# An attention kernel with its side work re-planned: second norms in two parts, tokens copied out of PSUM, pieces gathered beside the GELU

## The chip, the cores and the metric

The kernel runs on one core of a Trainium2 chip. The metric is the device time of one execution in microseconds (us). Three executions of the kernel before took 2359.71, 2360.52 and 2369.72 us; the median is 2360.52.

## The reference

The input `x` holds 8 waveforms (the batches) of 120000 samples, each cut into 1500 frames of 80. D is 256, everything is float32. Cut to what is computed:

```python
h = layernorm(einsum('bfr,hr->bfh', frames, W) + b) * gamma + beta
h = gelu(h)                                    # tokens, 8 x 1500 x 256
z = layernorm(h)
Q, K, V = heads(z @ Wq.T + bq), heads(z @ Wk.T + bk), heads(z @ Wv.T + bv)  # 16 heads of 16
h = h + join(softmax(Q @ K.T / 4) @ V) @ Wo.T + bo         # 1500 x 1500 per head
t = layernorm(h)                               # the third stage takes 8 // 16 = 0 tokens
out = h + layernorm(t) * ln_g + ln_b           # per head, so its norm alone is left
```

## The kernel before

**Tiling.** A batch of 1500 tokens is 12 tiles (`NT`) of 125 (`T`) or 3 chunks (`NC`) of 500 (`QC`). The 16 heads form 4 groups of 4. A *unit* is one group of heads against one chunk of queries: 12 units a batch (u = 0 to 11), 96 in all. A unit has 24 *slots* (`WIN`, k = 0 to 23). In slot k TensorE computes the scores of slot k + 1, two heads against one tile of keys, into two PSUM banks of four (`scores`, L972), ScalarE takes the exponential of 125x1000 numbers (L537), and on even slots TensorE multiplies the probabilities of two finished slots into the attended heads (`attend`, L1002), two further banks.

**Side work.** Everything else is cut into *pieces* that a table `PLAN[u, k]` puts into odd slots, written by hand with `place(u, what, (k, i), ...)`. A piece with several steps takes a step every second slot (`OFFSETS`). The pieces are: `tok` i, two tiles of tokens of a later batch; `turn` i, transposes of two tiles of z; `qk` i, a projection of one chunk to Q (even i) or K (odd i), i below 6 for the first two groups of heads, from 6 on for the last two; `norm` and `flag`, sums of squares and a bound for the softmax's scale; `val` i, values of a tile; `out` i, the output projection of a tile of the batch in front. TensorE runs them in `beside` (L1006). Pieces of units 5 to 11 mostly belong to the next batch. All pieces of a unit use one pair of PSUM banks, the pair in which the unit in front gathered its attended heads. So a piece waits until VectorE has freed the piece in front of it (`s_free`), and the first piece of a unit waits until `take_sums` has read the pair (`s_ov`).

**VectorE** goes through the same table, in order: in slot 1 `take_sums` (L669, L671), in slot 7 `invert` (L675), in slot 12 `normalise` (L679, L681), and for the last step of each piece `tok_stats` and `tok_norm` (L567 to L583), `take_turn` (L608), `take_qk` (L619, L621: the float16 high and low half), `take_val` (L628), `take_norm`, `take_flag` (L643 on) and `take_out` (L688 to L694), whose end `finish_out` (L702) follows three slots later. After `take_sums` the second norm of the next batch stands at the places in `NORMS`: `norm_stats` (L591, L594), then a wait for the root that GpSimd computes (L408, L410), then `norm_apply` (L600), one chunk at a time.

**ScalarE** takes the GELU of the next batch, all twelve tiles, at unit 4, slot 2 (`GELU`), with a table load in front and behind; TensorE has nothing in its program for that time.

**SP** issues the DMAs, in one order too: the sums go out to a thin layout (`spread_sums`, L300, slot 1) and back as reciprocals (`gather_sums`, L304, slot 7); four stores bring the attended heads to `oT` (`store_attended`, L315, slot 12); the halves of a projection go to DRAM (L281) and come back in the layout that scores need by eight loads (`lay_out`, L295), three slots later. Before the first unit of each half batch TensorE waits for those loads (`laid_out`).

**The start** makes the tokens of batch 0 and its first six projections with whole pieces, four pairs of banks in turn; VectorE takes all of them, and ScalarE is idle after its GELUs until the first scores.

## Time and profile before

| | |
|---|---|
| median of three executions | 2360.52 us |
| the profiled execution | 2361.47 us, of which its span is 2359.7 |
| ScalarE busy | 2134.5 us (90%) |
| TensorE busy | 2080.5 us (88%) |
| VectorE busy | 963.5 us (41%) |
| GpSimd busy | 394.8 us (17%) |
| TensorE's mean granted clock | 0.966 |
| chain that ended last | ScalarE 40%, TensorE 27%, issue 13%, VectorE 7% |

Times in the rows count from the start of the span. A group of instructions has its busy time, its mean in ns, and the idle time of its engine before it with what ended most of it. Busy shares are means over all stages. Where two engines are both near 90%, the question is which waits for which, and in which unit.

### The profile page before, as it was taken

To read this page: it belongs to the slowest core of one execution; us is meant where nothing else is said; L and a number is where in the kernel's file an instruction comes from. 1 tells how busy PE (TensorE), PEld (TensorE's weight loads), DVE (VectorE), ACT (ScalarE), POOL (GpSimd) and SP (SyncE) were. 2 spreads that over 40 slices of the span, in tenths; PEclk is the share of its full clock that TensorE was granted. 3 is DMA by queue.
4 is the path that set the end of the run, shared out by engine and by line. 5 is a ranking of instruction groups with operands and counts; after the bars stand their busy time and mean duration, and the time that the engine had idled before them with its cause. 6 is when DMAs were issued, how large, how long until landed. Compare 5 with 4: busy or idle time off the path is not lost.

```text
span 2359.7 us, 123320 instructions
## 1 busy us (share of the span) xinstructions
PE 2080.5 (88%) x56576; PEld 902.7 (38%) x56576; DVE 963.5 (41%) x2261; ACT 2134.5 (90%) x2334; POOL 394.8 (17%) x637
## 2 busy tenths in 40 slices
PE   4798999889998899988999799998999889999885
PEld 1432444333433344433444344443444333433223
DVE  6443335452344424444345433454335453343214
ACT  1498999989999899998999899998999989999993
POOL 2211102130122201222012210222102130011003
PEclk7998999999999999999999999999999999999997
DMA  2311211212121120221212112121211203122001
GB/s 71 81 45 42 56 42 46 56 31 75 32 57 48 44 67 22 59 64 43 62 25 57 53 48 58 35 58 38 66 41 48 53 23 78 28 58 57 18 10 35
DMA packets 114866, 113.91 MB, mean 48 GB/s; under 512 B 41003, under 2 KB 110698, under 8 KB 114338
## 3 DMA queue, kind: packets, MB, share of 16 engines
q1 hardware_dynamic: 111802, 104.10, 17.3%
q8 instruction: 446, 7.31, 1.3%
q10 hardware_dynamic: 2536, 1.83, 0.3%
q14 instruction: 82, 0.67, 0.1%
HBM read 55.16 MB, written 36.86 MB: 39 GB/s over the span
## 4 chain that ended last, share of the span: by engine, by line
ACT 40%; PE 27%; issue 13%; DVE 7%; SPq 5%; DMA 4%; POOL 2%; DVEq 2%; POOLq 0%
ACT prob L537 39%; PE PS L1002 12%; PE PS L972 7%; SPq L295 3%; DMA qk_halves_scratch<-HL 3%; PE PS L924 2%; SPq L315 1%; PE PS L871 1%; PE PS L909 1%; PE PS L894 1%; DMA oT<-Osb 1%; DVE Hs L576 1%; DVE z L600 1%; DVE Den L679 1%; POOL Hs L418 1%
## 5 line engine op out<-in xcount | busy, mean ns | idle before, releaser
L537 ACT ACTIVATE prob<-PS 125x1000 f32<-125x1000 f32 x2304 | 2089.7, 1070 | 155.9 <-PE PS L972 151.2
L1002 PE MATMUL PS<-prob,Vst 64*17 64x500 f32 (+1 forms) x18432 | 1214.7, 587 | 1.6 <-issue 0.8
L972 PE MATMUL PS<-QA,KA 64*32 64x500 f16 (+1 forms) x18432 | 958.9, 381 | 132.4 <-ACT prob L537 124.5
L972 PEld LDWEIGHTS PS<-QA,KA 64*32 64x32 f16 (+1 forms) x18432 | 276.8, 90 | 1054.0 <-ACT prob L537 1004.2
L1002 PEld LDWEIGHTS PS<-prob,Vst 61*17 61x17 f32 (+1 forms) x18432 | 341.3, 93 | 42.2 <-issue 9.0
L619 DVE TENSOR_SCALAR HL<-PS,b_qk 128x500 f16<-128x500 f32 x96 | 70.9, 739 | 459.4 <-PE PS L894 453.2
L894 PE MATMUL PS<-zT,w_qk 64*32 64x250 f32 x5760 | 229.4, 372 | 15.0 <-DVE Hs L576 8.5
L426 POOL TENSOR_TENSOR sq<-HL 128x500 bf16<-128x500 f16 x96 | 98.1, 1022 | 861.1 <-DVE HL L621 761.1
L924 PE MATMUL PS<-w_o,oT 64*32 64x128 f32 (+1 forms) x6144 | 129.9, 279 | 38.7 <-DVE Hs L576 27.9
L433 POOL TENSOR_TENSOR Y<-Hs,be_ln 125x256 f32<-125x256 f32 x96 | 70.3, 732 | 540.3 <-DVE Hs L688 529.5
L909 PE MATMUL PS<-w_v,zT 64*32 64x128 f32 (+1 forms) x5376 | 116.9, 280 | 34.2 <-DVE nrow L643 33.6
L894 PEld LDWEIGHTS PS<-zT,w_qk 64*32 64x32 f32 x5760 | 107.5, 106 | 70.8 <-DVE Hs L576 12.1
L924 PEld LDWEIGHTS PS<-w_o,oT 64*32 64x32 f32 (+1 forms) x6144 | 99.8, 108 | 88.6 <-DVE Hs L576 41.5
L909 PEld LDWEIGHTS PS<-w_v,zT 64*32 64x32 f32 (+1 forms) x5376 | 91.8, 109 | 66.2 <-DVE nrow L643 36.8
L688 DVE TENSOR_TENSOR Hs<-Hs,PS 125x256 f32<-125x256 f32 x96 | 40.3, 420 | 186.9 <-PE PS L924 186.9
L669 DVE COPY Osb<-PS 128x500 f32<-128x500 f32 x96 | 64.5, 672 | 117.9 <-PE PS L1002 116.4
L628 DVE TENSOR_TENSOR Vst<-PS,b_v 125x256 f32<-125x256 f32 x96 | 39.8, 419 | 160.4 <-PE PS L909 159.5
L871 PE MATMUL PS<-w_tok,X 40*32 40x256 f32 (+3 forms) x1536 | 68.2, 405 | 13.6 <-DMA w_tok<-in_tok_b 9.5
L418 POOL TENSOR_TENSOR Hs<-Hs,b_o 125x256 f32<-125x256 f32 x96 | 71.5, 775 | 31.4 <-DVE z L600 31.4
L675 DVE RECIPROCAL thin<-thin 100x20 f32<-100x20 f32 x96 | 26.5, 276 | 119.8 <-DMA thin<-Osb 119.8
L621 DVE SCALAR_TENSOR_TENSOR HL<-PS,b_qk,HL 128x500 f16<-128x500 f32 x96 | 71.0, 739 | 7.5 <-issue 0.4
L681 DVE TENSOR_TENSOR Osb<-Den,Osb 128x500 f32<-128x500 f32 x96 | 68.3, 712 | 7.5 <-issue 0.4
(83 smaller groups left out, 968.9 us busy)
## 6 DMA issues: line engine op xcount, KB each, us to landing
qk_halves_scratch<-HL SPq DMA_DIRECT2D x96, 250.0 KB, 2.3
QA<-qk_halves_scratch SPq DMA_DIRECT2D x384, 62.5 KB
KA<-qk_halves_scratch SPq DMA_DIRECT2D x384, 62.5 KB
oT<-Osb SPq DMA_DIRECT2D x384, 31.2 KB, 2.0
out<-Y SPq DMA_DIRECT2D x24, 500.0 KB
X<-in_x SPq DMA_DIRECT2D x16, 234.4 KB
thin<-Osb SPq DMA_DIRECT2D x96, 7.8 KB
Den<-thin SPq DMA_DIRECT2D x96, 7.8 KB
```

Of the source, the lines that this page charges most:

```text
L295: sp.dma_start(dst[to:to + HD, 2 * m:2 * m + 2, :, k * QC:(k + 1) * QC], src[par])\
L418: ins = pool.tensor_tensor(h, h, b_o[:, :], ALU.add)
L426: pool.tensor_tensor(sq[:, p % 2, :], HL[:, p % 3, 0, :], HL[:, p % 3, 0, :], ALU.mult).then_inc(s_sq, 1)
L537: act.activation(prob[0:T, 2 * (w % 6):2 * (w % 6) + 2, :], PS[0:T, 2 * (w % 2):2 * (w % 2) + 2, 0:QC], ACT.Exp, scale=scl)\
L619: dve.tensor_scalar(hi, both, bias, None, ALU.add)
L621: dve.scalar_tensor_tensor(out=lo, in0=both, scalar=bias, in1=hi, op0=ALU.add, op1=ALU.subtract)\
L871: last = pe.matmul(PS[lo:hi, bank + j, 0:D], X[rows, 2 * i + j, lo:hi], w_tok[rows, :], start=(step == 0), stop=(step == 1))
L894: last = pe.matmul(PS[lo:hi, bank + j, 0:QC // 2], w_qk[rows, c, w, m * 128 + lo:m * 128 + hi], zT[rows, c, k * QC + j * QC // 2:k * QC + ...
L909: last = pe.matmul(PS[lo:hi, bank + j, 0:D // 2], zT[rows, c, t + lo:t + hi], w_v[rows, c, j * D // 2:(j + 1) * D // 2], start=(step == 0 ...
L924: last = pe.matmul(PS[lo:hi, bank + j, 0:D // 2], oT[rows, c, oslot(b, e // CT), e % CT * T + lo:e % CT * T + hi], w_o[rows, c, j * D // 2 ...
L972: last = pe.matmul(PS[lo:hi, bank, 0:QC], KA[rows, G % NG, h // 2, t * T + lo:t * T + hi], QA[rows, G % NG, h // 2, c * QC:(c + 1) * QC], ...
L1002: last = pe.matmul(PS[lo:lo + HD + 1, bank + r, 0:QC], Vst[rows, b % 2, t, g * HG + j, :], prob[rows, (HG * t + j) % 12, :], start=(t == 0 ...
```

## The change

- The norm is split: `norm_stats` and the root in `STATS`, `norm_apply` and the bias in `APPLY`, with slots between them, in units 4 and 5.
- Tokens of batches after the first are copied from PSUM to SBUF first, which frees the banks; statistics and the subtraction read the copy.
- `gather_in` puts outputs 9 and 10 and projection 11, all steps, into the even slot 2 of unit 4, where the GELU stands. `beside` is now called in every slot, after `attend`.
- Most other pieces change place. Outputs 0 to 3 are all in unit 11, tokens 0 and 1 in units 9 and 10, turns in units 4 and 5.
- `lay_out` of finished projections is issued in slot 13, after the stores of attended heads, no longer three slots after the projection.
- At the start ScalarE takes the turns' copies and the high halves, with a semaphore for each (`s_zt`, `s_hi`), and issues the loads of odd projections. `FREED` counts the pieces that VectorE frees, since these turns no longer count in `s_free`.

The diff, without the semaphores' bookkeeping: everywhere else `s_free` is waited for with `FREED[n]` instead of `n`.

```diff
+    def gather_in(u, k, what, *at):
+        for i in at:
+            for step in range(len(OFFSETS[what])):
+                PLAN[u, k].append((what, i, step, step == len(OFFSETS[what]) - 1))
+    GELU = (4, 2)
+    STATS = {(4, 5): 0, (4, 10): 1, (4, 18): 2}
+    APPLY = {(4, 8): 0, (4, 17): 1, (5, 4): 2}
     place(0, "qk", (3, 6), (17, 7))
-    place(0, "out", (13, 3))
+    place(0, "out", (13, 4))
     place(1, "norm", (3, 3))
-    place(1, "out", (5, 4), (13, 5))
+    place(1, "out", (5, 5), (13, 6))
     place(1, "tok", (9, 2))
     place(1, "qk", (17, 8))
-    place(2, "out", (5, 6), (13, 7))
+    place(2, "out", (5, 7), (13, 8))
     place(2, "tok", (9, 3))
     place(2, "qk", (17, 9))
     place(3, "norm", (3, 4))
-    place(3, "tok", (5, 4), (13, 5))
-    place(3, "out", (9, 8))
+    place(3, "tok", (5, 4), (11, 5))
     place(3, "qk", (17, 10))
-    place(4, "out", (5, 9), (9, 10))
-    place(4, "qk", (17, 11))
+    gather_in(4, 2, "out", 9, 10)
+    gather_in(4, 2, "qk", 11)
+    place(4, "out", (7, 11))
+    place(4, "turn", (13, 0), (15, 1), (21, 2), (23, 3))
     place(5, "norm", (3, 5))
-    place(5, "turn", (5, 0), (7, 1))
-    place(5, "out", (9, 11))
-    place(5, "flag", (13, 1))
-    place(5, "val", (15, 0), (19, 1))
-    place(6, "turn", (3, 2), (5, 3))
-    place(6, "qk", (7, 0), (17, 1))
+    place(5, "flag", (7, 1))
+    place(5, "turn", (9, 4), (11, 5))
+    place(5, "val", (13, 0), (17, 1), (21, 2))
+    place(6, "qk", (3, 0), (17, 1))
+    place(6, "val", (13, 3))
     place(7, "norm", (3, 0))
-    place(7, "val", (5, 2), (13, 3))
-    place(7, "turn", (9, 4), (11, 5))
+    place(7, "val", (5, 4), (9, 5), (13, 6))
     place(7, "qk", (17, 2))
-    place(8, "qk", (3, 3), (17, 4))
-    place(8, "val", (13, 4))
+    place(8, "val", (5, 7), (9, 8), (13, 9))
+    place(8, "qk", (17, 3))
     place(9, "norm", (3, 1))
-    place(9, "val", (5, 5), (9, 6), (13, 7))
-    place(9, "qk", (17, 5))
-    place(10, "norm", (3, 2))
-    place(10, "val", (5, 8), (11, 9), (15, 10), (19, 11))
-    place(10, "flag", (9, 0))
-    place(11, "tok", (3, 0), (11, 1))
-    place(11, "out", (7, 0), (15, 1), (19, 2))
-    assert all(len(steps) < 1 + k % 2 for (u, k), steps in PLAN.items())
-    NORMS = {(4, 12): 0, (5, 12): 1, (6, 8): 2}
-    GELU = (4, 2)
+    place(9, "val", (5, 10), (9, 11))
+    place(9, "tok", (13, 0))
+    place(9, "qk", (17, 4))
+    place(10, "tok", (5, 1))
+    place(10, "qk", (17, 5))
+    place(11, "norm", (3, 2))
+    place(11, "out", (5, 0), (13, 1), (17, 2), (21, 3))
+    place(11, "flag", (9, 0))
+    assert all(len(steps) < 1 + k % 2 or (u, k) == GELU for (u, k), steps in PLAN.items())
...
-            return b + 2 if u >= NU - 2 else b + 1
+            return b + 2 if u >= NU - 3 else b + 1
...
+    FREED, TURNED = [0], [0]
+    for what, pb, i in USE:
+        turned = (what, pb) == ("turn", 0)
+        FREED.append(FREED[-1] + (not turned))
+        TURNED.append(TURNED[-1] + turned)
...
+        def lay_out(eng, b, i):
+            p, k, w, m = nth(b, i), chunk_of(i), i % 2, i // (2 * NC)
+            dst = KA if w else QA
+            eng.wait_ge(s_st[p % 3], at(s_st[p % 3], 16 * (p // 3 + 1)))
+            if p >= 4 * NC or second[0]:
+                eng.wait_ge(s_sc, at(s_sc, max(0, WIN * NC * 2 * (p // (2 * NC) - 1))))
+            for par in range(2):
+                for blk in range(4):
+                    to, half_ = 64 * par + HD * blk, blk // 2 if w else blk % 2
+                    src = qk_s[b, i, :, half_, :].rearrange("(a two r) q -> two r a q", two=2, r=HD)
+                    eng.dma_start(dst[to:to + HD, 2 * m:2 * m + 2, :, k * QC:(k + 1) * QC], src[par])\
+                      .then_inc(s_ld, 16)
...
                 for i in range(2 * NC):
                     store_halves(0, i)
-                    if i > 0:
-                        lay_out(0, i - 1)
-                lay_out(0, 2 * NC - 1)
+                    if i % 2:
+                        lay_out(sp, 0, i - 1)
...
-                        if stored and stored[0][0] == WIN * n + k:
-                            lay_out(*stored.pop(0)[1:])
...
                         if k == NORMALISE + 1:
+                            while stored:
+                                lay_out(sp, *stored.pop(0))
                             if u == 4 and b + 2 < B:
                                 load_x(b + 2)
-                            if u in (1, 3, 6) and b > 0:
-                                store_out(b - 1, u // 2 if u < 6 else 2)
+                            if u in (0, 2, 5) and b > 0:
+                                store_out(b - 1, (u + 1) // 2 if u < 5 else 2)
...
-                                stored.append((WIN * n + k + 3, pb, i))
+                                stored.append((pb, i))
...
+                            if b + 1 < B and (u, k) in STATS:
+                                root2(b + 1, STATS[u, k])
+                            if b + 1 < B and (u, k) in APPLY:
+                                add_bias(b + 1, APPLY[u, k])
...
+            def turn_out(i):
+                act.wait_ge(s_full, at(s_full, USE["turn", 0, i] + 1))
+                bank = pair(USE["turn", 0, i])
+                act.activation(zT[:, :, i * 2 * T:(i + 1) * 2 * T], PS[:, bank:bank + 2, 0:2 * T], ACT.Copy)\
+                   .then_inc(s_zt, 1)
+            def high_half(i):
+                p, w, bank = nth(0, i), i % 2, pair(USE["qk", 0, i])
+                if p >= 3 or second[0]:
+                    act.wait_ge(s_st[p % 3], at(s_st[p % 3], 16 * (p // 3)))
+                    act.wait_ge(s_sq, at(s_sq, max(0, p - 2)))
+                act.wait_ge(s_full, at(s_full, USE["qk", 0, i] + 1))
+                act.activation(HL[:, p % 3, 0, :].rearrange("p (a q) -> p a q", a=2), PS[:, bank:bank + 2, 0:QC // 2],
+                               ACT.Identity, bias=b_qk[:, w * KC:w * KC + 1]).then_inc(s_hi, 1)
...
+                for k in range(NC):
+                    for j in range(2 * k, 2 * k + 2):
+                        turn_out(j)
+                    for i in range(2 * k, 2 * k + 2):
+                        high_half(i)
+                        if i > 0 and i % 2 == 0:
+                            lay_out(act, 0, i - 1)
+                lay_out(act, 0, 2 * NC - 1)
...
+            def fresh(b, i):
+                return Hs[:, hslot(b, 2 * i):hslot(b, 2 * i) + 2, :]
             def tok_stats(b, i):
                 p, tok = i % 2, two(USE["tok", b, i], slice(0, T), D)
                 dve.wait_ge(s_full, at(s_full, USE["tok", b, i] + 1))
+                if b > 0:
+                    dve.tensor_copy(fresh(b, i), tok).then_inc(s_free, 1)
+                    dve.drain()
+                    tok = fresh(b, i)
...
+                if b > 0:
+                    tok = fresh(b, i)
...
-                ins.then_inc(s_free, 1)
+                if b == 0:
+                    ins.then_inc(s_free, 1)
...
-                if p >= 3 or second[0]:
+                if (p >= 3 or second[0]) and p >= 2 * NC:
                     dve.wait_ge(s_st[p % 3], at(s_st[p % 3], 16 * (p // 3)))
...
-                dve.tensor_scalar(hi, both, bias, None, ALU.add)
+                if p < 2 * NC:
+                    dve.wait_ge(s_hi, at(s_hi, p + 1))
+                else:
+                    dve.tensor_scalar(hi, both, bias, None, ALU.add)
...
+                    if b + 1 < B and (u, k) in STATS:
+                        norm_stats(b + 1, STATS[u, k])
+                    if b + 1 < B and (u, k) in APPLY:
+                        norm_apply(b + 1, APPLY[u, k])
...
-                    if finish and finish[0][0] == k:
+                    if finish and finish[0][0] <= k:
...
-                    for j in range(2):
-                        take_turn(0, 2 * k + j)
...
+            def turned(b, i):
+                if b == 0:
+                    pe.wait_ge(s_zt, at(s_zt, i + 1))
+                else:
+                    pe.wait_ge(s_free, at(s_free, FREED[USE["turn", b, i] + 1]))
...
-                        pe.wait_ge(s_free, at(s_free, use))
+                        pe.wait_ge(s_free, at(s_free, FREED[use]))
...
-                    if k % 2:
-                        beside(b, u, k)
-                    elif k:
+                    if k % 2 == 0 and k:
                         attend(n, k // 2 - 1)
-                    elif n > 0:
+                    elif k == 0 and n > 0:
                         attend(n - 1, NT - 1)
+                    beside(b, u, k)
...
-                    pe.wait_ge(s_free, at(s_free, use - reach + 1))
+                    pe.wait_ge(s_free, at(s_free, FREED[use - reach + 1]))
+                    if use < FIRST and TURNED[use - reach + 1]:
+                        pe.wait_ge(s_zt, at(s_zt, TURNED[use - reach + 1]))
```

## Rows read from the trace of the kernel before

**Rows 1.** Costliest groups: line, operation, count | busy, mean ns | idle before, releaser

```profile
L537 ACT ACTIVATE prob<-PS 125x1000 f32<-125x1000 f32 x2304 | 2089.7, 1070 | 155.9 <-PE PS L972 151.2
...
L619 DVE TENSOR_SCALAR HL<-PS,b_qk 128x500 f16<-128x500 f32 x96 | 70.9, 739 | 459.4 <-PE PS L894 453.2
```

**Rows 2.** Timeline of ScalarE, last batch: start us, length us, what, [idle before]

```profile
2089.71 230.17 ACT L537 ACTIVATE prob<-PS 125x1000 f32<-125x1000 f32 x256 [0.43 <-PE PS L972]
```

**Rows 3.** ScalarE's windows of units 1+2, 3+11, 4, 5, 7, batches 0-6: sums

```profile
sum 315.91, ACT 304.60; mean ACT 21.76
...
sum 326.87, ACT 307.14; mean ACT 21.94
...
sum 200.96, ACT 190.40; mean ACT 27.20
...
sum 202.32, ACT 155.03; mean ACT 22.15
...
sum 165.76, ACT 154.39; mean ACT 22.06
```

**Rows 4.** The same for units 0, 6, 8, 9 and 10 together

```profile
605.63:627.39 21.76, 21.71 (x25) 1.00 0.18 46
...
sum 761.76, ACT 756.47; mean ACT 21.61
```

**Rows 5.** Timeline of ScalarE at the GELU of batch 1

```profile
459.36 1.28 ACT L530 ACT_TABLE_LOAD   x1
...
464.82 3.69 ACT L537 ACTIVATE prob<-PS 125x1000 f32<-125x1000 f32 x4
```

**Rows 6.** Timeline of VectorE and TensorE, batch 1, unit 5

```profile
500.46 1.40 DVE L591 BATCH_NORM_STATS2 st<-Hs 125x6 f32<-125x256 f32 x4
...
503.86 1.38 DVE L600 TENSOR_SCALAR z<-Hs,mv,rs 125x256 f32<-125x256 f32 x4 [1.55 <-POOL rs L410]
...
505.42 1.11 PE L909 MATMUL PS<-w_v,zT 64*32 64x128 f32 x32 [5.10 <-DVE nrow L643]
```

**Rows 7.** Timeline of VectorE and TensorE behind a token piece, batch 1, unit 1

```profile
399.98 0.77 DVE L567 BATCH_NORM_STATS2 st<-PS 125x6 f32<-125x256 f32 x2 [0.86 <-PE PS L871]
...
402.09 0.67 PE L924 MATMUL PS<-w_o,oT 64*32 64x128 f32 x32 [0.88 <-DVE Hs L576]
...
404.56 0.42 DVE L688 TENSOR_TENSOR Hs<-Hs,PS 125x256 f32<-125x256 f32 x1
...
405.51 0.64 PE L894 MATMUL PS<-zT,w_qk 64*32 64x250 f32 x16
...
405.85 0.48 DVE L694 SCALAR_TENSOR_TENSOR hg<-Hs,mv,g_ln 125x256 f32<-125x256 f32 x1
```

**Rows 8.** Timeline of TensorE behind the GELU of batch 1

```profile
465.88 0.61 PE L972 MATMUL PS<-QA,KA 64*32 64x500 f16 x8 [5.24 <-ACT prob L537]
```

**Rows 9.** Timeline of VectorE, a turn's copy at the start

```profile
44.13 0.68 DVE L608 COPY zT<-PS 128x500 f32<-128x500 f32 x1 [0.15 <-PE PS L880]
```

**Rows 10.** Timeline of VectorE, the sums' second step, batch 1, unit 4

```profile
460.13 0.68 DVE L671 TENSOR_TENSOR Osb<-Osb,PS 128x500 f32<-128x500 f32 x1
```

**Rows 11.** Timeline of VectorE, normalise in batch 1, unit 10

```profile
618.21 0.01 DVE L679 LOAD_MASK_SELECT Den<-Den  x1 [1.83 <-DMA Den<-thin]
...
619.01 0.68 DVE L681 TENSOR_TENSOR Osb<-Den,Osb 128x500 f32<-128x500 f32 x1
```

**Rows 12.** Timeline of SP's issues: start, last to first scores, stores, loads

```profile
83.24 3.70 SPq L295 DMA_DIRECT2D KA<-qk_halves_scratch  x8
...
404.60 2.45 SPq L315 DMA_DIRECT2D oT<-Osb  x4
...
610.01 6.20 SPq L295 DMA_DIRECT2D KA<-qk_halves_scratch  x8
```

**Rows 13.** Loads by line L295: engine, times as min/median/max ns

```profile
L295 SPq DMA_DIRECT2D QA<-qk_halves_scratch x384: 302/426/2057, 53.1 to 2158.9; - x192
```

**Rows 14.** Timeline of TensorE, the first scores

```profile
88.81 1.03 PE L972 MATMUL PS<-QA,KA 64*32 64x500 f16 x16 [7.57 <-DMA KA<-qk_halves_scratch]
```

More of the change, by code:

```diff
@@ L887, in project @@
                 if step == 0:
-                    pe.wait_ge(s_free, at(s_free, USE["turn", b, 2 * k + 1] + 1))
+                    turned(b, 2 * k + 1)
                 begin("qk", b, i, step)
@@ L901, in values @@
                 if step == 0:
-                    pe.wait_ge(s_free, at(s_free, USE["turn", b, i // 2] + 1))
+                    turned(b, i // 2)
                 begin("val", b, i, step)
@@ L1106, in run @@
                 pe.wait_ge(s_wo, 16 * 5)
[L1107 removed]
+                pe.wait_ge(s_free, at(s_free, FREED[FIRST]))
                 for b in range(B):
```

34 lines of the change are left out of this document (8 added, 26 removed).

## The prediction

> **What bounds the kernel now.** I read the costliest groups of the page first. ScalarE computes 2304 exponentials that cover 2089.7 us of the 2359.7 us span, and almost all of its idle time there, 151.2 us, is waiting for TensorE's scores (L972) [rows 1]. So ScalarE sets the pace, and the question is what a unit of 24 exponentials costs against its floor. The floor is in the last batch, where 256 exponentials run without a gap in 230.17 us, 0.899 each, 21.58 a unit [rows 2]. Next I cut ScalarE's time into units, the same unit of batches 0 to 6 together, and took the floor (7 x 21.58 = 151.05, twice that for a pair of units) from each sum [rows 3, 4]. Lost in seven batches: units 1 and 2 together 13.8 us, units 3 and 11 together 24.8, unit 4 12.3 (after 7 x 5.37 for GELU and its two table loads: 5.46 from 459.36 to 464.82 [rows 5], less 0.09 that the last exponential in front saves in overlap), unit 5 51.3, unit 7 14.7, and the five others 6.5. That is 123 us. The last batch loses nearly nothing. The start, up to the first scores, is looked at by itself; the tail behind the last exponential is not touched. These 123 us are all that the middle can give.
>
> The cause of each loss is in the timelines of TensorE and VectorE. In unit 5 TensorE stands 5.10 us before a value piece, because VectorE is in the second norm (statistics, 1.55 us waiting for GpSimd's root, application) and reaches the flag row only then [rows 6]. TensorE then works at half clock (1.11 us for a half piece of values). After every token piece it stands 0.88 us, since the two PSUM banks come free only after statistics and subtraction [rows 7]; there are six token pieces a batch, two each in units 3 and 11, one each in 1 and 2. At the GELU TensorE is idle for 5.24 us [rows 8] and starts again at half clock.
>
> **The change part by part.** I follow one batch, in the frame of batch 1, with the durations of its rows.
>
> *Unit 5.* Norm statistics and application are split and moved to units 4 and 5, so that the root is ready when VectorE comes back, and flag and turns no longer follow a norm. Between the pieces left in unit 5 VectorE has under 2 us of work each. Of 51.3 I leave 1.4: -49.9.
>
> *Unit 7.* There two turns were mixed with values, and the sums were spread behind eight loads on SP. Now it holds values (one 0.4 us VectorE step each), and the loads come after the attended heads. Of 14.7 I leave 0.5: -14.2.
>
> *Tokens.* A copy of two banks costs about 0.68 [rows 9] and frees them after 0.8 us instead of 2.1. The price is 0.68 more on VectorE for each pair. In unit 3 and in units 9 and 10, where the pieces of unit 11 go, the next piece is four slots off or VectorE has room: the token stalls of units 3 and 11 go, of their 24.8 I leave 1 (-23.8), to which unit 11's new wait is added below. In units 1 and 2 the order stays token, normalise, output, projection. From the start of statistics (399.98) to the freeing of the output piece (L688 ends 404.98) VectorE takes 5.0 us [rows 7]; with the copy 5.7. TensorE wants that pair for the projection 4.65 us after the same point (it came at 405.51, 5.53 later, and 0.88 of that is the wait that now goes). So it waits 1.1 us one piece later, where it waited 1.1 before: 13.8 becomes 13.3 (-0.5). On reading from SBUF: four statistics from SBUF take 1.40 us, 0.35 each [rows 6], two from PSUM 0.77 [rows 7], 0.38 each, so the copy earns back at most 0.1 us.
> The Trainium skill (VectorE: DVE Perf Modes, "The TRN2 errata") charges a VectorE instruction 58 cycles plus its elements from SBUF and 120 from PSUM, at 0.96 GHz; by that, four later reads would earn back an estimated 0.26 us and units 1 and 2 would end some 3 us lower. The row speaks for less.
>
> *The burst at GELU.* Slot 2 of unit 4 now holds outputs 9 and 10 and projection 11, in one row, on one pair of banks. TensorE can start when the sums are taken, 460.8 [rows 10]. An output piece is two steps of 0.65, a projection four of 0.64 [rows 7]; each next piece waits about 0.6 for VectorE's take of 0.42. 460.9 + 1.35 + 0.6 + 1.3 + 0.6 + 2.6 = 467.4. Scores for the fifth exponential of the unit then come at 467.4 rather than when the bank is free (465.9), so ScalarE waits about 1.15 us, but at full clock; before, the slow restart cost most of unit 4's 1.76 (12.3 over 7).
> Behind it VectorE carries a backlog: take 11 (L619 and a second step like it, 0.74 each [rows 1]) to 469.2, statistics 1.8 to 471.1, two finishes 1.0, reciprocal 0.3, application 1.4 from the root at 472.7 to 474.1, output 11 1.8 (as L688 to the end of L694 [rows 7]), statistics 1.8, normalise 1.5, a finish 0.5: 479.6, and only then turn 0, whose banks TensorE wants for turn 1 at 478.3. Free at 480.3: a wait of 2.0, of which 1.85 reaches ScalarE. So unit 4 costs 3.1 us in batches 1 to 6 and about 0.8 in batch 0 (no outputs yet): 19.4 for 12.3, +7.1. Bounds 12 and 30: no backlog at all, or each application with the 2 us that it has beside GpSimd work.
> In batch 7 the same three pieces stand in slot 2 with no GELU above them. TensorE leaves the slot 6.7 us late and nothing hides it: +6.7.
>
> *Loads behind attended heads.* This is a new wait. Projection 5 of the next batch ends at slot 23 of unit 10, and its eight loads go out at slot 13 of unit 11, in SP's order behind the four stores of attended heads, which wait for VectorE's normalise. In unit 10 of before (starts 605.63 [rows 4]) normalise began at 618.21, 1.83 of it waiting for the sums' DMA [rows 11], which now is not behind loads. With an output instead of a value (+0.3) and a finish (+0.5) it ends 13.0 us after the unit's start. Stores 2.45, loads 4.6 (6.2 in the longest group [rows 12], 3.4 if all eight take the median of 0.43 [rows 13]), landing 1.9 (the last issue before the first scores ended at 86.94, the scores began at 88.81 [rows 12, 14]): 22.0. TensorE wants them 20.8 us in. So each of seven hand-overs waits 1.2 us, of which 1.1 counts, 7.7, with small stalls +8.2. Bounds: 0 and 2.7 each, 19 in all. For units 6 to 11 the loads go out in unit 4, early enough.
>
> *The start.* ScalarE takes turn copies and high halves, VectorE the low halves. Equal cost, but eight loads are issued on ScalarE between high halves 2 and 3, and again between 4 and 5. No row shows loads issued there; I take SP's 4.6 for eight, 3.4 and 6.2 as its ends. High half 3 slips by 3 us, and with it norm, turns and projection 4, high half 5 by 6. Against that the last loads no longer queue behind five others: TensorE waited 7.57 us for them [rows 14]. My chain gives the last landing at 89.3 for 88.8: +0.5, bounds -2 and +4.
> The Trainium skill (DMA: Bandwidth & Descriptors, "Issuing engines are not separate DMA queues") says that a second issuing engine saves only the issuing time. That is all that I count here.
>
> The other five units: -1 (one token stall in batch 0). Sum: -49.9 -14.2 -23.8 -0.5 +7.1 +6.7 +8.2 +0.5 -1.0 = -66.9. The profiled execution took 2361.5 (span 2359.7 and 1.8 around it), the median is 0.95 lower: 2360.5 - 67 = 2294 with rounding.
>
> **Rivals.** (A) The clock falls in the burst. TensorE pauses four times for banks while the sequence runs. At half clock a half piece costs 1.11 [rows 6] instead of 0.65; eight steps make 3.8 us a batch, some 26 in all: 2320. For it: the clock did fall after 5.24 us idle. Against it: no pause in the burst is over 0.7 us, and after the pause of 0.88 us the output step took 0.67, full speed [rows 7].
> The Trainium skill (TensorE: Matmul & The Clock Gate, "A second HAM failure mode: psum-queue depth-cycling") has this very case, short idles between groups that wait for PSUM banks. By that rule this rival would hold.
> (B) VectorE becomes the bound wherever a copy was added, as I expect it in units 1 and 2 only: units 3, 9 and 10 would then keep the 1 us per token piece, four a batch, and the turns wait 2 us in batch 0 too: +28 +2, 2324. Against it: there the pieces stand four slots apart.
> (C) The change does not do what it says: the unit 5 stall is the flag's own chain (take, transposes), not the norm in front. Then about 4 of 7.3 us stay: 2294 + 28 = 2322. The rows speak against it: the norm ends at 505.24, and TensorE starts at 505.42 [rows 6].
> (D) Slower: loads right behind the stores fill the ring. The longest single load issue lasted 2.06 us [rows 13]. If all eight took that, the hand-over would come 16.5 - 4.6 = 11.9 us later, 83 us in seven, and the time is 2377. It decides from 11.3 us each (67 + 12 = 79 over 7). Only single loads were that slow, so it is unlikely.
>
> **How the numbers follow.** Forecast 0.62, A 0.12, B 0.1, C 0.06, in between or a stall that I have not seen 0.06, D 0.04. The forecast's own bounds: down 7 (unit 4), 8 (hand-over) and 2 (start); up 11, 11 and 4. Not all at once: 2278 to 2310. The range takes in A, B and C: 2277 to 2326. A measurement can tell about 0.5%, 12 us, from no change. Faster by over that 0.91, within 0.05, slower 0.04.
>
> **What would show it.** Right: in unit 5 ScalarE's windows sum to 153 rather than 202 and no 5 us wait before a value piece; in unit 3 no idle between token and next piece; in units 1 and 2 the idle has moved from the output to the projection; one gap of 6 to 7 us in batch 7, unit 4; a wait for turn 0's banks in unit 4; TensorE waits for KA or QA at the end of unit 11. A shows as half clock (1.2 GHz) in the stretch behind GELU. I am wrong if VectorE's chain with the copy is not 5.7 us, or if the loads need clearly more or less than 4.6.

## The result, and the profile after

The changed kernel took 2303.92 us (median of 4 executions, 2301.73 to 2309.14), the kernel before 2360.11 beside it: a ratio of 0.9757 (95% interval 0.9726 to 0.9788), 56 us less. The forecast was 2294 in a range of 2277 to 2326, and faster. The profiled execution took 2301.73 (2361.47 before): 59.7 less, where the sum said 66.9. So the time fell in the range, and 7 to 10 us of the forecast gain are missing.

The page after. Columns are those of [rows 1]: busy time, mean in ns, idle time before and what ended most of it.

```profile
span 2299.7 us, 123422 instructions
PE 2071.1 (90%) x56576; PEld 871.5 (38%) x56576; DVE 974.5 (42%) x2291; ACT 2131.7 (93%) x2346; POOL 393.4 (17%) x637
...
ACT 51%; PE 22%; issue 10%; DVE 6%; SPq 3%; POOL 2%; DMA 2%; DVEq 2%; POOLq 1%; ACTq 0%
...
L579 ACT ACTIVATE prob<-PS 125x1000 f32<-125x1000 f32 x2304 | 2079.5, 1086 | 69.3 <-PE PS L1034 66.7
```

ScalarE's idle time ahead of the exponentials (L537 before, L579 now) fell from 155.9 to 69.3 us, of which TensorE's scores end 66.7. Some 38 of that fall is no gain: ahead of the first exponential the row counts 49.7 us before and 11.2 after, since ScalarE now has work at the start, while that exponential came only 1.4 us sooner. The other 48 lie between the exponentials, and their busy time fell by 10 (from 2089.7), as one that follows a stop takes longer: 1.00 us alone and about 0.91 in a row. The number of exponentials is the same, and ScalarE's part in the chain that ended last rose from 40% to 51%. VectorE has 11 us more to do: its 42 token copies take 28.6, and against them stand the six turn copies and six high halves that went to ScalarE (8.5) and smaller differences.

ScalarE's windows of batches 0 to 6, cut as in [rows 3, 4]: units 1 and 2, units 3 and 11, unit 4, unit 5, unit 7, then the five others. The first number is the length of all windows together, to be set against the floor of 151.05 a unit.

```profile
sum 313.06, ACT 304.38; mean ACT 21.74
...
sum 317.39, ACT 303.38; mean ACT 21.67
...
sum 212.16, ACT 192.63; mean ACT 27.52
...
sum 154.39, ACT 152.70; mean ACT 21.81
...
sum 151.85, ACT 151.64; mean ACT 21.66
...
sum 759.92, ACT 753.61; mean ACT 21.53
```

Less the floor, and 37.6 for GELU and tables in unit 4, beside the sum of the prediction (differences are taken before rounding). "Hand-over" is the wait at the end of unit 11 for the loads that the next batch's first scores need:

| term | before | after | measured | predicted |
|---|---|---|---|---|
| unit 5 | 51.3 | 3.3 | -47.9 | -49.9 |
| unit 7 | 14.7 | 0.8 | -13.9 | -14.2 |
| units 3 and 11 (tokens go, hand-over comes) | 24.8 | 15.3 | -9.5 | -23.8 + 8.2 |
| units 1 and 2 | 13.8 | 11.0 | -2.8 | -0.5 |
| unit 4, batches 0 to 6 | 12.3 | 23.5 | +11.2 | +7.1 |
| unit 4, batch 7 | 0 | 7.1 | +7.1 | +6.7 |
| the five others | 6.5 | 4.7 | -1.8 | -1.0 |
| first exponential | 89.5 | 88.1 | -1.4 | +0.5 |

With -1.0 in the rest of batch 7 and in the tail these make the 60.0 by which the span fell. A window of one unit alone, unit 3, sums to 151.17: of 15.3 in units 3 and 11, 15.2 is the hand-over in unit 11. Two terms are too small in the forecast, hand-over by 7 and unit 4 by 4, and the five others hide a stall that was not foreseen: unit 0 rose from 2.8 to 7.3 over eight batches, while the rest fell.

The granted clock changed too. Before, TensorE fell to half clock (1.2 GHz) once in unit 4 and once in unit 5 of batches 0 to 6; the mean of those windows was 0.88 or 0.89 (0.94 in unit 5 of two batches), as in batch 1's unit 5:

```profile
485.80:515.36 29.56, 22.22 (x26) 0.88 0.14 35
```

After, both units stand at 1.00 in every batch. So what unit 5 gained is the wait and the slow restart behind it.

What stands behind each, in timelines (start, length, idle before and its end). Batch 1, unit 4, on ScalarE behind the GELU and its table load (to 450.62), then TensorE's burst and VectorE beside it:

```profile
450.63 1.90 ACT L579 ACTIVATE prob<-PS 125x1000 f32<-125x1000 f32 x2
454.01 11.83 ACT L579 ACTIVATE prob<-PS 125x1000 f32<-125x1000 f32 x13 [1.48 <-PE PS L1034]
```

```profile
446.67 1.47 PE L986 MATMUL PS<-w_o,oT 64*32 64x128 f32 x64 [0.22 <-DVE Osb L728]
448.72 1.46 PE L986 MATMUL PS<-w_o,oT 64*32 64x128 f32 x64 [0.58 <-DVE Hs L745]
450.76 3.00 PE L956 MATMUL PS<-zT,w_qk 64*32 64x250 f32 x64 [0.58 <-DVE Hs L745]
```

The pauses between the three pieces are 0.58 us, as the 0.6 of the prediction; a piece of output takes 1.47 rather than 1.35 and the projection 2.8 up to the next scores (453.55), not 2.6. So the exponentials wait 1.48 here and at most 1.57 in batches 1 to 6, not 1.15. The granted clock through the burst was 1.00, which is 2.4 GHz:

```profile
447.00:451.00 4.00, 2.58 (x132) 1.00 0.03 6
451.00:455.00 4.00, 3.63 (x96) 1.00 0.02 4
```

(window, its length, TensorE busy, granted clock, DMA share, GB/s). Rival A needed half clock there and falls.

Unit 4 loses 3.84 us in each of batches 1 to 6: this wait, 1.6 ahead of turn 1, which waits for turn 0's banks (forecast 1.85), and some 0.7 that is in neither. ScalarE's own busy time is 27.5 to 27.6 a unit there, where floor and GELU make 26.95 (27.2 before). The runs don't take that part apart.

In batch 7 there is no GELU above the burst, and in unit 1 the wait moved to the projection:

```profile
2094.91 5.49 ACT L579 ACTIVATE prob<-PS 125x1000 f32<-125x1000 f32 x6 [7.07 <-PE PS L1034]
```

```profile
387.74 0.69 DVE L614 COPY Hs<-PS 125x512 f32<-125x512 f32 x1 [0.74 <-PE PS L927]
388.52 0.75 DVE L618 BATCH_NORM_STATS2 st<-Hs 125x6 f32<-125x256 f32 x2
...
393.01 0.41 DVE L745 TENSOR_TENSOR Hs<-Hs,PS 125x256 f32<-125x256 f32 x1
```

```profile
393.48 0.66 PE L956 MATMUL PS<-zT,w_qk 64*32 64x250 f32 x16 [0.92 <-DVE Hs L745]
```

From the start of the copy (387.74) to the end of the step that frees the output's pair (393.42) VectorE takes 5.7 us, which is the 5.7 of the prediction, and TensorE waits 0.92 for it. No other token piece has a wait over 0.5 us behind it.

The hand-over at the end of batch 1's unit 11, which starts at 603.7 (VectorE, SP, TensorE; the scores feed unit 0 of the next batch):

```profile
616.23 0.68 DVE L738 TENSOR_TENSOR Osb<-Den,Osb 128x500 f32<-128x500 f32 x1
```

```profile
616.94 3.27 SPq L332 DMA_DIRECT2D oT<-Osb  x4
620.31 4.59 SPq L299 DMA_DIRECT2D KA<-qk_halves_scratch  x8
```

```profile
626.78 0.40 PE L1034 MATMUL PS<-QA,KA 64*32 64x500 f16 x8 [1.58 <-DMA KA<-qk_halves_scratch]
```

Normalise ends 13.2 us into the unit here, 12.9 to 13.5 in the seven (13.0 forecast). The four stores took 3.27, 3.0 in the mean (2.45 forecast), the eight loads 4.59 here, but 4.5 to 6.4 in the seven and 5.0 in the mean (4.6 forecast). The scores start 23.1 us into the unit here and 23.3 in the mean, where the chain gave 22.0. TensorE waits 1.58 us for them here, 1.2 to 3.2 in the seven; the longest wait stands behind the longest loads (batch 4).

The stall in unit 0 that was not in the sum, batch 1 (VectorE, then TensorE):

```profile
355.63 0.48 DVE L751 SCALAR_TENSOR_TENSOR hg<-Hs,mv,g_ln 125x256 f32<-125x256 f32 x1
356.58 0.48 DVE L759 SCALAR_TENSOR_TENSOR Y<-hg,rs,Y 125x256 f32<-125x256 f32 x1 [0.46 <-POOL rs L454]
357.01 0.68 DVE L726 COPY Osb<-PS 128x500 f32<-128x500 f32 x1
357.76 0.68 DVE L728 TENSOR_TENSOR Osb<-Osb,PS 128x500 f32<-128x500 f32 x1
```

```profile
358.49 0.66 PE L956 MATMUL PS<-zT,w_qk 64*32 64x250 f32 x16 [1.22 <-DVE Osb L728]
```

Output 3 has its second step in slot 23 of unit 11. Its take and its finish, which waits 0.46 us for GpSimd's root, stand on VectorE ahead of `take_sums`, and the first piece of unit 0 needs the pair that `take_sums` reads.

### The profile page after: what moved, and what is told of

Read it like the earlier page. It is cut to its first block, busy times and chain, and to the rows that moved or that the text cites. A ratio compares the mean times of both kernels' runs of the same rounds, so it can differ in the third digit from the quotient of the medians.

```text
span 2299.7 us, 123422 instructions
## 1 busy us (share of the span) xinstructions
PE 2071.1 (90%) x56576; PEld 871.5 (38%) x56576; DVE 974.5 (42%) x2291; ACT 2131.7 (93%) x2346; POOL 393.4 (17%) x637
## 4 chain that ended last, share of the span: by engine, by line
ACT 51%; PE 22%; issue 10%; DVE 6%; SPq 3%; POOL 2%; DMA 2%; DVEq 2%; POOLq 1%; ACTq 0%
ACT prob L579 51%; PE PS L1064 9%; PE PS L1034 5%; PE PS L956 2%; PE PS L986 2%; SPq L299 2%; DMA thin<-Osb 1%; PE PS L971 1%; SPq L332 1%; PE PS L936 1%; DVE Den L736 1%; DMA KA<-qk_halves_scratch 1%; DVE Hs L745 1%; DVEq L746 1%; DVEq L727 1%
## 5 line engine op out<-in xcount | busy, mean ns | idle before, releaser
L579 ACT ACTIVATE prob<-PS 125x1000 f32<-125x1000 f32 x2304 | 2079.5, 1086 | 69.3 <-PE PS L1034 66.7
L1064 PE MATMUL PS<-prob,Vst 64*17 64x500 f32 (+1 forms) x18432 | 1190.4, 580 | 0.7 <-ACT prob L579 0.6
L1034 PE MATMUL PS<-QA,KA 64*32 64x500 f16 (+1 forms) x18432 | 934.4, 377 | 121.9 <-ACT prob L579 107.5
L1034 PEld LDWEIGHTS PS<-QA,KA 64*32 64x32 f16 (+1 forms) x18432 | 263.7, 89 | 1086.6 <-ACT prob L579 1054.8
L1064 PEld LDWEIGHTS PS<-prob,Vst 61*17 61x17 f32 (+1 forms) x18432 | 333.5, 93 | 35.8 <-issue 4.5
L450 POOL TENSOR_TENSOR Y<-Hs,be_ln 125x256 f32<-125x256 f32 x96 | 70.5, 734 | 437.7 <-DVE Hs L745 437.7
L986 PE MATMUL PS<-w_o,oT 64*32 64x128 f32 (+1 forms) x6144 | 125.3, 275 | 17.4 <-DMA oT<-Osb 9.0
L956 PEld LDWEIGHTS PS<-zT,w_qk 64*32 64x32 f32 x5760 | 101.5, 105 | 89.3 <-DVE Hs L745 22.5
L986 PEld LDWEIGHTS PS<-w_o,oT 64*32 64x32 f32 (+1 forms) x6144 | 95.4, 107 | 50.8 <-issue 10.7
L971 PE MATMUL PS<-w_v,zT 64*32 64x128 f32 (+1 forms) x5376 | 110.5, 269 | 0.6 <-issue 0.6
L435 POOL TENSOR_TENSOR Hs<-Hs,b_o 125x256 f32<-125x256 f32 x96 | 68.2, 743 | 78.5 <-DVE z L654 78.5
L927 PE MATMUL PS<-w_tok,X 41*32 41x256 f32 (+3 forms) x1536 | 65.5, 408 | 13.6 <-DMA w_tok<-in_tok_b 9.9
```

Source lines behind the costliest of these rows:

```text
L435: ins = pool.tensor_tensor(h, h, b_o[:, :], ALU.add)
L450: pool.tensor_tensor(Y[:, k % 2, e % CT, :], Hs[:, hslot(b, e), :], be_ln[:, :], ALU.add)
L579: act.activation(prob[0:T, 2 * (w % 6):2 * (w % 6) + 2, :], PS[0:T, 2 * (w % 2):2 * (w % 2) + 2, 0:QC], ACT.Exp, scale=scl)\
L956: last = pe.matmul(PS[lo:hi, bank + j, 0:QC // 2], w_qk[rows, c, w, m * 128 + lo:m * 128 + hi], zT[rows, c, k * QC + j * QC // 2:k * QC + ...
L971: last = pe.matmul(PS[lo:hi, bank + j, 0:D // 2], zT[rows, c, t + lo:t + hi], w_v[rows, c, j * D // 2:(j + 1) * D // 2], start=(step == 0 ...
L986: last = pe.matmul(PS[lo:hi, bank + j, 0:D // 2], oT[rows, c, oslot(b, e // CT), e % CT * T + lo:e % CT * T + hi], w_o[rows, c, j * D // 2 ...
```

## The experiments

All kernels below compute everything. "Unit sums" are what ScalarE loses against the floor in that unit, added over the eight batches; for the changed kernel, units 0 to 5 and 11: 7.3, 5.8, 5.0, 0.0, 30.6, 3.3, 15.3. They scatter where an edit can't reach: unit 11 lost 13.1 to 18.5 in the kernels that leave its pieces and loads alone, and batch 0's units 0 and 4 vary by 1 to 2.5 us with a fall to half clock that some executions have there. The kernel before took 2357.86, 2360.48 and 2358.54 us beside the three groups of runs.

### Without the copy of the tokens

```diff
-                if b > 0:
-                    dve.tensor_copy(fresh(b, i), tok).then_inc(s_free, 1)
-                    dve.drain()
-                    tok = fresh(b, i)
...
```

> The changed kernel without the copy of the tokens: statistics and subtraction read PSUM again. Theory (spacing): what took the token stalls out of unit 3 is that the next piece stands four slots behind the token, not the copy. Without the copy a wait of 1 us comes back only where the next piece is two slots off and VectorE's queue is short: unit 9 in six batches, and twice in batch 0; in units 1 and 2 the wait moves from the projection back to the output at the same size. 2304 + 8 = 2312 us. Rival (copy, as the prediction had it): units 3 and 9 to 11 get their waits back, four a batch, some 2330 us.

Measured 2318.21 us, ratio 0.9829 (0.9794 to 0.9863). Units 1 and 2 lose the same with and without the copy (5.7 and 4.8); without it TensorE waits one piece earlier, at the output:

```profile
399.11 0.67 PE L979 MATMUL PS<-w_o,oT 64*32 64x128 f32 x32 [0.87 <-DVE Hs L623]
```

Unit 3 goes from 0.0 to 3.8, unit 9 from -0.5 to 5.1. That is 9.4 us by the copy. Start, hand-over and unit 4, which this edit should not touch, add 1.8, 2.5 and 2.2, and unit 0 adds 2.0, all of it in batch 0 (2.0 for -0.2; four kernels that keep the copy lose 1.1 to 1.3 there), so of the 14 us between the medians some are scatter. I had unit 9 in my 8, and not unit 3. Of the 13.3 us that unit 3 lost before, 3.8 come back without the copy; the other 9.5 went with its new plan, which spaces the pieces and has one output less. The prediction had put all under one term, without a share for either.

### The split alone, in the kernel before

```diff
-    NORMS = {(4, 12): 0, (5, 12): 1, (6, 8): 2}
+    STATS = {(4, 12): 0, (5, 8): 1, (6, 6): 2}
+    APPLY = {(4, 15): 0, (5, 11): 1, (6, 9): 2}
...
```

A split can't leave both halves in place: the applications move by one to three slots, the statistics by up to four.

> The kernel before with the norm split alone: statistics at slots (4,12), (5,8), (6,6), application at (4,15), (5,11), (6,9), everything else as it was. Theory (norm in front of the flag): VectorE reaches the flag at 501.6 in the frame of batch 1 instead of 505.2, TensorE waits 1.6 us instead of 5.1 and keeps its clock; unit 5 loses 10 us in seven batches instead of 51: 2360 - 41 = 2319 us. Rival (the flag's own chain and the turns hold TensorE): some 4 of 7.3 us a batch stay, 2338 us.

Measured 2330.37 us, 0.988 (0.9844 to 0.9916). Unit 5 falls from 51.2 to 19.4, so the second norm in front was about 32 of the 48 us that the whole change took out there, and the flag's own chain (rival C) at most the rest. The slow restart went with the long wait: the granted clock in unit 5 is 1.00 in six of seven batches, for 0.88 to 0.94 before. What is left is again VectorE's order, shown in batch 1 by the application and the flag row:

```profile
493.71 1.38 DVE L602 TENSOR_SCALAR z<-Hs,mv,rs 125x256 f32<-125x256 f32 x4 [1.55 <-POOL rs L411]
...
498.60 0.20 DVE L645 COPY nrow<-PS 1x64 f32<-1x64 f32 x1
```

```profile
498.86 0.67 PE L912 MATMUL PS<-w_v,zT 64*32 64x128 f32 x32 [1.79 <-DVE nrow L645]
```

The 1.55 us for GpSimd's root are still waited for with three slots between the halves. Application, a take of output and normalise then stand ahead of the flag row. The split needs the new places to be worth all of it.

### The new places, norms whole

```diff
-    STATS = {(4, 5): 0, (4, 10): 1, (4, 18): 2}
+    STATS = {(4, 8): 0, (4, 17): 1, (5, 4): 2}
```

Statistics now stand in the slot of their application.

> The changed kernel with the norm whole again: statistics at the slots of the applications, (4,8), (4,17), (5,4), so VectorE waits 1.5 us for each root. Theory (place counts, split little): in unit 5 the flag comes four slots after the norm, so only 0.7 us a batch comes back there, and about 1.4 us before turn 2 in unit 4, less 0.6 that turn 0 gains: 2304 + 9 = 2313 us. Rival (the split itself removed the stall of unit 5): 5 us a batch come back in unit 5, 2339 us.

Measured 2337.86 us, 0.9912 (0.9885 to 0.994). I was wrong: not 9 but 34 us over the changed kernel. Unit 5 loses 12.5 (3.3 with the split), but unit 4 takes most, 53.6 for 30.6. VectorE, GpSimd and ScalarE of batch 2:

```profile
743.89 1.38 DVE L654 TENSOR_SCALAR z<-Hs,mv,rs 125x256 f32<-125x256 f32 x4 [1.54 <-POOL rs L427]
...
750.44 0.48 DVE L759 SCALAR_TENSOR_TENSOR Y<-hg,rs,Y 125x256 f32<-125x256 f32 x1 [1.57 <-POOL rs L454]
```

```profile
745.35 2.98 POOL L435 TENSOR_TENSOR Hs<-Hs,b_o 125x256 f32<-125x256 f32 x4 [1.50 <-DVE z L654]
748.29 1.16 POOL L450 TENSOR_TENSOR Y<-Hs,be_ln 125x256 f32<-125x256 f32 x1
...
749.86 0.55 POOL L454 TENSOR_TENSOR rs<-rs,mhalf 125x1 f32<-125x1 f32 x1
```

```profile
753.09 1.00 ACT L579 ACTIVATE prob<-PS 125x1000 f32<-125x1000 f32 x1 [4.27 <-PE PS L1034]
```

A second cost of a late application shows here. Behind it GpSimd adds the bias (L435) for 2.98 us, then output 11's own addition (L450, 1.16 us), and only then comes the root of output 11 (L454). VectorE stands 1.57 us in `finish_out` for this root, and turn 0 is next on VectorE. No run takes the root ahead of L450. TensorE's wait for turn 0, 3.8 us, also brought it to half clock: unit 4's windows stand at 0.94 or 0.95 here and at 1.00 in the changed kernel, so a part of the 23 us of unit 4 is the slow restart.

### Who holds turn 0 in unit 4

```diff
-    STATS = {(4, 5): 0, (4, 10): 1, (4, 18): 2}
+    STATS = {(4, 5): 0, (4, 14): 1, (4, 18): 2}
```

The prediction saw turn 0 behind VectorE's backlog: here the second statistics (1.8 us) go behind turn 0.

> The changed kernel with the second chunk's statistics at (4,14) instead of (4,10), behind turn 0 on VectorE. Theory (backlog in front of turn 0): the wait of 1.7 us at slot 17 of unit 4 goes in six batches: 2304 - 10 = 2294 us. Rival (VectorE is short of time in the whole unit): the 1.8 us are missing at turn 2 or at the sums of unit 5 instead, 2304 us.

Measured 2302.64 us, 0.9764 (0.9736 to 0.9791): no gain. The rival had the time right, but not the cause: nothing went missing at turn 2 or in unit 5 (2.5 for 3.3), the wait for turn 0's banks stayed where it was. VectorE, GpSimd and ScalarE of batch 2:

```profile
738.29 1.08 DVE L738 TENSOR_TENSOR Osb<-Den,Osb 128x500 f32<-128x500 f32 x1
740.95 0.48 DVE L759 SCALAR_TENSOR_TENSOR Y<-hg,rs,Y 125x256 f32<-125x256 f32 x1 [1.58 <-POOL rs L454]
741.35 0.67 DVE L662 COPY zT<-PS 128x500 f32<-128x500 f32 x1
```

```profile
738.80 1.17 POOL L450 TENSOR_TENSOR Y<-Hs,be_ln 125x256 f32<-125x256 f32 x1
...
740.37 0.55 POOL L454 TENSOR_TENSOR rs<-rs,mhalf 125x1 f32<-125x1 f32 x1
```

```profile
743.13 3.85 ACT L579 ACTIVATE prob<-PS 125x1000 f32<-125x1000 f32 x4 [1.72 <-PE PS L1034]
```

VectorE had nothing to do for 1.58 us and waited for GpSimd's root. So my backlog was only one of two holders of equal length. The next kernel keeps this edit and moves the finish of output 11 behind turn 0 too:

```diff
-                            finish.append((k + 3, pb, i))
+                            finish.append((k + 5 if u == 4 and i == NT - 1 else k + 3, pb, i))
```

> The changed kernel with the second chunk's statistics at (4,14) as in the run before, and with the finish of output 11 two slots later (slot 14, behind turn 0). Theory (GpSimd's queue): output 11's root waits on GpSimd behind the 3 us of the first chunk's bias, VectorE waits for that root in its finish, and turn 0 stands behind the finish. With the finish behind turn 0 and the statistics too, nothing is in front of it: the wait of 1.8 us at slot 17 of unit 4 goes in six batches, 2303 - 10 = 2293 us. Rival (VectorE's own instructions, normalise above all, end too late anyway): it stays, 2303 us.

Measured 2295.18 us, 0.9732 (0.9713 to 0.9751); unit 4 falls from 31.4 (with the statistics moved alone) to 22.1. In batches 1 to 6 it is 1.8 us each in all but one (3.97 to 2.14), as expected; batch 0 gives 1.1 back, with half clock behind its GELU. Turn 0's copy now follows the normalise:

```profile
738.68 1.08 DVE L738 TENSOR_TENSOR Osb<-Den,Osb 128x500 f32<-128x500 f32 x1
739.69 0.67 DVE L662 COPY zT<-PS 128x500 f32<-128x500 f32 x1
```

The wait for GpSimd's root is shown as the second holder. The pair of edits gains; the finish without the statistics was not run.

### The burst of three outputs, and its copy in batch 7

```diff
-    gather_in(4, 2, "out", 9, 10)
-    gather_in(4, 2, "qk", 11)
-    place(4, "out", (7, 11))
+    gather_in(4, 2, "out", 9, 10, 11)
+    place(4, "qk", (3, 11))
...
+                            if len(finish) == 2:
+                                finish_out(*finish.pop(0)[1:])
```

> The changed kernel with outputs 9, 10 and 11 beside the GELU and projection 11 in slots 3 to 9, of unit 4. Theory (length of the burst): three outputs need 1.3 + 0.6 + 1.3 + 0.6 + 1.3 = 5.1 us from 460.9, so TensorE is back at 466.0 when the bank is free; the wait at slot 4 shrinks from 1.7 to 0.3 in six batches and from 7.3 to 5.7 in batch 7, and VectorE has 1 us less of backlog before turn 0: 2304 - 8 - 2 - 5 = 2289 us. Rival (VectorE's three output chains bind): the banks come free later, projection 11 waits, and the unit costs what it did: 2304 us.

Measured 2295.59 us, 0.9731 (0.9704 to 0.9759). Unit 4 falls from 30.6 to 20.6. After the tables ScalarE waits 0.43 us and not 1.48 (batch 1):

```profile
459.27 2.86 ACT L578 ACTIVATE prob<-PS 125x1000 f32<-125x1000 f32 x3
462.56 8.33 ACT L578 ACTIVATE prob<-PS 125x1000 f32<-125x1000 f32 x9 [0.43 <-PE PS L1035]
```

Two things changed at once: the burst is 1.3 us shorter, and output 11 is out of the way of turn 0, behind which ScalarE waits 0.44 to 0.62 us and no longer 1.6. Batches 1 to 6 lose 1.9 each for 3.84, batch 7 6.3 for 7.1; batch 0 loses 2.4 more, at half clock. Each of the two waits fell by 1.0 to 1.2. The medians differ by 8.3 us, for 10 in unit 4.

The last batch with its four pieces spread over slots 3 to 21 again:

```diff
...
+        for what, i, step, last in SPREAD.get(k, []) if (b, u) == (B - 1, 4) else PLAN[u, k]:
```

> The changed kernel, where the last batch, which has no GELU, runs outputs 9 to 11 and projection 11 of unit 4 in odd slots (3, 7, 11 and 15 on), and only there. Theory (uncovered burst): the gap of 7.1 us in batch 7, unit 4 goes and nothing else moves: 2297 us. Rival (the work costs the same wherever it stands): 2304 us.

Measured 2297.82 us, 0.9741 (0.9706 to 0.9776). Batch 7's unit 4 loses 0.02 us instead of 7.11: the uncovered burst is what the forecast said, in size and place.

### Loads of the hand-over sooner

```diff
+                        if u == NU - 1 and k == 2 and stored:
+                            lay_out(sp, *stored.pop(0))
```

> The changed kernel, where the loads of projection 5 go out in slot 2 of unit 11 instead of slot 13 behind the stores of attended heads; all other loads stay. Theory (late loads): TensorE no longer waits for them at the end of unit 11, which cost 15 us over seven batches between units 11 and 0: 2290 us. The wait before the first piece of unit 0 (1.1 us a batch) stays, since it comes from output 3 at slot 21. Rival (order on SP pays elsewhere): the eight loads hold the sums' second DMA back by 4 us, normalise ends later, and half of the gain is lost: 2298 us.

Measured 2289.3 us, 0.9715 (0.968 to 0.975). Unit 11 falls from 15.3 to 1.9. This is the hand-over term, shown alone: 13.4 us for SP's order, where the forecast had 8.2. Unit 0 kept its stall (8.6), so delay by the hand-over is not needed for it; the place of output 3 is enough.

```diff
-    place(11, "out", (5, 0), (13, 1), (17, 2), (21, 3))
+    place(11, "out", (5, 0), (11, 1), (15, 2), (19, 3))
```

> The changed kernel with outputs 1, 2 and 3 of unit 11 two slots earlier (11, 15, 19). Theory (output 3 holds the sums): the wait of 1.1 us before the first piece of unit 0 goes, seven times; the hand-over stays: 2304 - 7 = 2297 us. Rival (the first piece waits for the sums' own matmuls, held back by the hand-over): no change, 2304 us.

Measured 2298.12 us, 0.974 (0.9711 to 0.9769). Outputs 1 and 2 moved with it. Unit 0 falls from 7.3 to 0.1: the cause of the unforeseen stall is shown. Unit 11 reads 3.0 more, 18.3, which is inside its scatter (18.5 with only the last batch changed).

### Token last in units 1 and 2

```diff
-    place(1, "out", (5, 5), (13, 6))
-    place(1, "tok", (9, 2))
+    place(1, "out", (5, 5), (9, 6))
+    place(1, "tok", (13, 2))
```

and the same in unit 2.

> The changed kernel with the second output of units 1 and 2 in slots 9 and 11 and the token in 13 and 15, so the order is output, normalise, token, projection. Theory (the copy only moves the wait while token, normalise and output stand in a row on VectorE): the banks come free 0.8 us after the token's matmuls, the projection at slot 17 finds them free, and the 1 us a unit goes in both units: 2304 - 11 = 2293 us. Rival (VectorE lacks the time in these units whatever the order): the wait moves to the end of the unit or to the sums, 2304 us.

Measured 2293.49 us, 0.9717 (0.97 to 0.9735). Units 1 and 2 fall from 5.8 and 5.0 to 0.4 and -0.3. Normalise and the token's norm no longer stand together ahead of a piece that TensorE wants.

### The start as before

```diff
-                for k in range(NC):
-                    for j in range(2 * k, 2 * k + 2):
-                        turn_out(j)
-                    for i in range(2 * k, 2 * k + 2):
-                        high_half(i)
-                        if i > 0 and i % 2 == 0:
-                            lay_out(act, 0, i - 1)
-                lay_out(act, 0, 2 * NC - 1)
...
```

VectorE takes the turns and the high halves of the start again, and SP issues all of its loads.

> The changed kernel with the start of the kernel before: VectorE copies the turns and makes both halves, SP issues all loads in the old order. Theory (no net gain, as the prediction summed it): the loads issued on ScalarE hold high halves back by what the shorter queue on SP gives back, the first exponential stays at 88 to 92 us: 2304 us, within 2. Rival (8 us less work on VectorE in the start count): 2308 us or more.

Measured 2305.22 us, 0.977 (0.9753 to 0.9787), first exponential at 90.0. The part "more on ScalarE at first" is worth nothing that can be told. Nor can the 1.4 us by which the first exponential came sooner in the changed kernel be put down to it: kernels with the same start as the changed one began at 88.1 to 91.9. Their granted clock in the first microseconds differs, but does not order them: the changed kernel (1.00) and the one with output 3 sooner (0.78) both began at 88.1, the one with three outputs (0.78 too) at 91.9. The cause of the scatter stays open. The first two (windows as above):

```profile
0.00:42.00 42.00, 15.81 (x208) 1.00 0.28 75
```

```profile
0.00:42.00 42.00, 14.64 (x208) 0.78 0.27 75
```

### Together

The last batch spread, the early loads, output 3 sooner, three outputs in the burst, the second statistics behind turn 0 and the token last, in one kernel.

> All that helped or should help together: early loads of projection 5, the last batch's pieces in odd slots, outputs of unit 11 two slots earlier, three outputs beside the GELU with projection 11 behind, the second statistics at (4,14), tokens last in units 1 and 2. Theory (the waits are separate): 15 us at the hand-over, 7 in unit 0, 11 in units 1 and 2, 17 of unit 4's 31 (6 of them in batch 7) go: 2304 - 50 = 2254 us. Rival (VectorE has become the bound, what goes in one place comes back in another): half of it, 2279 us.

Measured 2250.43 us, 0.953 (0.9509 to 0.9552): 108 us less than the kernel before beside it, 53 less than the changed one (2303.92). Its row on the page, and its windows as above for units 1 and 2, units 3 and 11, unit 4 and unit 5:

```profile
L585 ACT ACTIVATE prob<-PS 125x1000 f32<-125x1000 f32 x2304 | 2075.6, 1091 | 20.5 <-PE PS L1042 18.2
```

```profile
sum 301.27, ACT 301.27; mean ACT 21.52
...
sum 304.43, ACT 302.57; mean ACT 21.61
...
sum 199.37, ACT 193.64; mean ACT 27.66
...
sum 154.85, ACT 153.10; mean ACT 21.87
```

ScalarE loses 13.6 us in eight batches, 10.7 of it in unit 4 (66.2 and 30.6 in the changed kernel). Behind the GELU of batch 1, 207 exponentials follow each other without a stop:

```profile
453.55 187.48 ACT L585 ACTIVATE prob<-PS 125x1000 f32<-125x1000 f32 x207 [0.43 <-PE PS L1042]
```

## Why the prediction was right, and where it was off

**The bound.** Right. ScalarE sets the pace, and nearly all of the 60 us came out of its waits for scores, unit by unit.

**Unit 5 and unit 7.** Right in size (-47.9 and -13.9 for -49.9 and -14.2). The cause in unit 5, the norm ahead of the flag row, is shown by the split alone (32 of 51) and by the norms made whole again (unit 5 back from 3.3 to 12.5, unit 4 up by 23.0). Neither undoes all of it, so I can't give each part its share: places and split work together. I had taken the split as the smaller part; at the new places it is worth 34 us. For unit 7 no run was made: that its turns and the loads ahead of the sums cost the 13.9 us is argued from the plan and not shown, and which of the two did it stays open.

**Tokens.** Unit 3 lost nothing any more, by the new plan of the unit more than by the copy (9.5 and 3.8 of 13.3). The wait in units 1 and 2 moved to the projection, as forecast, at 0.9 for 1.1 us; the pair of units gained 2.8 and not 0.5: 0.8 of it in batch 0, the rest in stalls beside this wait that the sum had not listed. Rival B (VectorE bound wherever a copy was added) is false in units 3, 9 and 10. The step on reading from SBUF stands: two statistics took 0.75 from the copy and 0.77 from PSUM [rows 7], and over the whole trace one took 419 ns from the copy (84 of them) and 423 from PSUM (96, before).
The Trainium skill (VectorE: DVE Perf Modes, "The TRN2 errata") would have two statistics from SBUF shorter by twice 62 cycles at 0.96 GHz, an estimated 0.13 us. The rows differ by 0.02, the means by 0.01 for two, and the measurement decides.

**The burst.** The place and the size in batch 7 are right (7.1 for 6.7). In the other batches the term was mis-sized, +11.2 for +7.1. The wait behind the GELU was 1.5 to 1.6 for 1.15, because output pieces took 1.47 for 1.35 and the projection 2.8 for 2.6. Another 0.6 a batch lies in ScalarE's own busy time and had no term. The wait for turn 0's banks was 1.6 for 1.85, nearly right for half a reason, which is luck: VectorE's backlog was there, but GpSimd's late root alone would have held turn 0 as long, and only both edits together removed it. My chain had listed the application "from the root" but not what the bias add, and the output's own addition behind it, do to the next root.
Rival A is false: the granted clock stayed at 1.00 through pauses of 0.58, in unit 4 of all eight batches.
The Trainium skill (TensorE: Matmul & The Clock Gate, "A second HAM failure mode: psum-queue depth-cycling") describes short idles between groups that make the clock oscillate, in a kernel of bf16 matmuls with N=512, which is another case than this one. The trace does not agree here: 1.00 in both windows of the burst.

**Hand-over.** The mechanism was right and the term mis-sized: 15.2 in seven batches, inside the bound of 19, for 8.2. Normalise ended where I had it, within 0.1. The chain came out 1.3 us longer: stores took 3.0 for 2.45, as I had taken them from one group in the quiet middle, loads 5.0 for 4.6, and small gaps made the rest; from the last issue to the scores it was 1.8 to 1.9 as forecast, in all but one batch (2.8). TensorE wanted the loads 21.5 us in and not 20.8, so its wait was 1.8 for 1.2, and the unit lost 2.2. A wait of 1.2 us that is the difference of 22.0 and 20.8 moves by half or more when either chain is off by 3 to 6%, and I should have made more of that bound.

**Unit 0.** The step that failed. "The other five units: -1" took units 0, 6, 8, 9 and 10 together. I had followed the pieces that change place into the unit that takes them, and not across its end, where output 3 meets the next unit's `take_sums`. That the term still came out near (-1.8 for -1.0) is luck: over seven batches unit 0 lost 3.4 us more, and units 6, 8, 9 and 10, of which nothing was forecast, lost 5.2 less.

**The start.** Forecast +0.5, measured nothing that can be told from its own scatter of 88.1 to 91.9.

**The sum.** Too good by 6.9 us of span (60.0 for 66.9): unit 4 +4.1, hand-over and tokens +6.1, unit 5 and unit 7 +2.3, batch 7 +0.4, less 2.3 in units 1 and 2, 1.9 at the start and 1.8 elsewhere. Rival C is refuted in its size, and D did not occur: loads behind the stores took 5.0 us in the mean and 6.4 at most.

## What to carry to other kernels

When side work is re-planned beside a pace-setting engine, follow the first and the last moved piece across the borders of its slot row: the costs that were missed sat at the ends of units and in the queue of a third engine, GpSimd, not in the middle. A wait that is a small difference of two long chains is known no better than the chains, so give it the bound of their sum. And a part of the schedule that is hidden below other work in most iterations must be planned again for the one in which the cover is gone.
